# One attention and FP4 feed-forward layer on one core: a new order for the setup

## What is computed

```python
xn = (x - mean(x)) / sqrt(var(x) + 1e-5)            # by rows
q, k, v = split(xn @ w_attn + b_attn)               # 16 heads of 8
scores = q @ k.T / sqrt(8) + mask                   # mask: -log(1 + distance) ahead, -inf behind
attn = (softmax(scores) @ v) @ w_proj + b_proj
def fp4(t):                                         # blocks of 16 along the last axis
    scale = max(max(abs(block)) / 6, 1e-12)
    return grid[searchsorted(mid, abs(block / scale))] * sign * scale
h = silu(fp4(xn) @ fp4(w_gate).T) * (fp4(xn) @ fp4(w_up).T)
out = x + attn + fp4(h) @ fp4(w_down).T
```

## Time and profile before

| what | value |
|---|---|
| median of 3 runs | 626.64 us (626.51 to 628.41) |
| profiled execution, its own time | 626.35 us |
| its span, first to last instruction | 624.5 us |
| mean granted TensorE clock | 0.985 |
| busy PE, DVE, POOL, ACT | 564.4 (90%), 562.8 (90%), 537.4 (86%), 400.8 (64%) us |
| chain that ended last, by engine | PE 43%, POOL 32%, DVE 13%, ACT 7%, issue 4% |

### The profile page before, as it was taken

The page is one execution under the profiler, slowest core; times in us unless marked ns, Lnnn a source line. Parts: engine busy times, 40 slices in busy tenths (PEclk is TensorE's granted clock), DMA queues, the critical chain, the costliest instruction groups (busy, mean ns, idle before and its releaser), DMA issues.

```text
span 624.5 us, 11270 instructions
## 1 busy us (share of the span) xinstructions
PE 564.4 (90%) x3807; PEld 250.9 (40%) x3807; DVE 562.8 (90%) x1178; ACT 400.8 (64%) x857; POOL 537.4 (86%) x400
## 2 busy tenths in 40 slices
PE   6999779999999999999989899999989898989985
PEld 5576534444343334333333332342334242432322
DVE  6899998989999999999999999998989999997661
ACT  4576457566656475767667577666656667759782
POOL 7226987789899989999998999999998999998992
PEclk9999988999999999999999999999999999999997
DMA  5255341310000000200000000000000000000000
GB/s 148 74 137 114 119 83 51 78 43 36 2 2 3 0 2 10 86 1 2 2 0 2 19 1 1 2 2 1 1 2 1 19 0 2 1 2 1 1 2 17
DMA packets 14715, 16.66 MB, mean 27 GB/s; under 512 B 1594, under 2 KB 14171, under 8 KB 14243
## 3 DMA queue, kind: packets, MB, share of 16 engines
q1 hardware_dynamic: 14123, 15.70, 9.2%
q10 hardware_dynamic: 536, 0.26, 0.2%
HBM read 11.75 MB, written 4.01 MB: 25 GB/s over the span
## 4 chain that ended last, share of the span: by engine, by line
PE 43%; POOL 32%; DVE 13%; ACT 7%; issue 4%; ACTq 0%; POOLq 0%; DVEq 0%
POOL ring L802 25%; PE psum L1396 11%; PE psum L1354 9%; PE psum L1378 7%; DVE mxp L1135 7%; ACT ring L954 2%; POOL xw L820 2%; POOL xw L818 2%; PE psum L1331 2%; POOL xw L822 2%; PE psum L1312 2%; PE psum L1314 1%; PE psum L1320 1%; DVE ring L1162 1%; PE psum L1404 1%
## 5 line engine op out<-in xcount | busy, mean ns | idle before, releaser
L802 POOL TENSOR_TENSOR ring<-ring,dist 128x1024 f32<-128x1024 f32 (+3 forms) x223 | 438.4, 1996 | 31.7 <-ACT ring L954 31.3
L1135 DVE TENSOR_REDUCE mxp<-psum 128x1 f32<-128x512 f32 (+3 forms) x640 | 352.6, 598 | 20.5 <-PE psum L1354 11.4
L954 ACT ACTIVATE ring<-psum 128x512 f32<-128x512 f32 (+3 forms) x446 | 211.5, 528 | 101.5 <-PE psum L1381 51.9
L1354 PE MATMUL psum<-kop,qop 96*128 96x512 bf16 (+3 forms) x640 | 198.0, 352 | 7.3 <-DVE mxp L1135 5.3
L1378 PE MATMUL psum<-qop,kop 128*128 128x512 bf16 (+3 forms) x640 | 190.7, 349 | 6.2 <-DVE mxp L1135 3.7
L1396 PE MATMUL psum<-ring,vaug 128*32 128x512 f32 (+3 forms) x1280 | 151.5, 544 | 15.0 <-POOL ring L802 14.1
L1162 DVE TENSOR_TENSOR ring<-psum,dist 128x512 f32<-128x512 f32 (+3 forms) x194 | 115.7, 622 | 13.9 <-ACT psum L954 13.8
L954 ACT ACTIVATE psum<-psum 128x512 f32<-128x512 f32 (+3 forms) x194 | 99.5, 543 | 39.7 <-PE psum L1378 23.4
L1354 PEld LDWEIGHTS psum<-kop,qop 96*128 96x128 bf16 x640 | 57.2, 97 | 127.8 <-DVE mxp L1135 46.5
L1378 PEld LDWEIGHTS psum<-qop,kop 128*128 128x128 bf16 x640 | 59.7, 97 | 82.2 <-DVE mxp L1135 15.5
L1357 PE MATMUL psum<-tri_q,identb 128*128 128x128 bf16 x256 | 56.2, 221 | 0.0
(11 more groups left out here) (130 smaller groups left out, 490.2 us busy)
## 6 DMA issues: line engine op xcount, KB each, us to landing
kop<-parts_dram SPq DMA_DIRECT2D x9, 384.0 KB
qop<-parts_dram SPq DMA_DIRECT2D x9, 384.0 KB
parts_dram<-qpart SPq DMA_DIRECT2D x18, 128.0 KB, 2.8
xin<-_attn_hidden_states_dram SPq DMA_DIRECT2D x4, 256.0 KB, 4.7
ring<-inv_dram SPq DMA_DIRECT2D x1, 1024.0 KB, 4.9
out_dram<-xin SPq DMA_DIRECT2D x4, 256.0 KB, 2.3
parts_dram<-qpart SPq DMA_DIRECT2D x6, 96.0 KB
qop<-parts_dram SPq DMA_DIRECT2D x3, 192.0 KB
```

Source lines behind the costliest of these rows:

```text
L802: g_.tensor_tensor(slot(p)[:, :, 0:n], slot(p)[:, :, 0:n], both, ALU.mult).then_inc(weighed_pool, 1)
L954: a_.activation(scores if pair_vec[p] else slot(p)[:, e % 2, 0:n], scores, ACT.Exp, scale=SCALE).then_inc(exp_done, 1)
L1135: v_.tensor_reduce(mxp[:, u % 2, 4 * a + j, c - g:c - g + 1], bank(*o)[:, 0:n], AX_X, ALU.max).then_inc(max_used, 1)
L1354: ins = mm(bank(*o)[:, 0:n], qop[0:K_MAX, u // NQ % 2, h, P * a:P * (a + 1)], kop[0:K_MAX, h, k0:k0 + n], start=True, stop=(c != g))
```

## The change

1. **Square root first.** `qzero(0)` on ACT now needs `sqrt(0)`, so the root is ACT's first activation.
2. **Row scales once.** The four small instructions of `scale` run for chunk 0 of the order and once, 12 columns wide, for the other three. `scale` of chunks 2 and 3 of the order is then only the four that write rows.
3. **Rests in PSUM.** For the first chunk DVE's two subtractions and ACT's second part work on the product's PSUM bank in place of the SBUF tile `qc`.
4. **Scales padded.** `amax` and `sc` are 35 columns for each piece, and stage 1 always writes all 35 through a view of 5 by 7, from a flat 35. DVE clears `amax` once at the start.
5. **Order.** FP4 piece 0 waits for the last `rest`. The selection products of heads 1 to 3, `scale`, `dist` and `v` get other ranks, the first unit's maxima are walked head by head, FP4 stages 3 to 5 get a rank of their own, and the plan lets some DVE items start only after POOL's running one. `WARM` is 20 in place of 30.
6. **Clearings in quarters.** `qzero(1)` and `kfill` of chunks 1 to 3 are four ACT instructions each; POOL's clearing of the weights' tile comes last of its constants.

```diff
-WARM = 30
+WARM = 20
+DIST_RANK, V_RANK, SEL_RANK, SCALE_RANK = 8, 8, 4.3, 4.5
+PORT_RANK = 6.8
...
-    add("ACT", ("qzero", 0), 2700, 200, [], rank=0)
+    add("ACT", ("qzero", 0), 2700, 200, [("ACT", ("sqrt", 0))], rank=0)
...
+            needs += [("DVE", ("rest", 1, 1))] if n == k == 0 else []
...
-        for a in range(TPG):
-            for j in range(4):
+        for a, j in sorted(((a, j) for a in range(TPG) for j in range(4)), key=lambda o: o[1] if u == 0 else 0):
...
+        if engine == "DVE" and (kind == "fp4" and item[2] >= 3 or kind == "scale" or item[0:3:2] == ("rest", 1)):
+            now = max(now, clock["POOL"] if pool_busy[0] else 0)
...
-                    a_.activation(qpart[:, t, 1], rest(t), ACT.Identity).then_inc(part2_ready, 1)
+                    a_.activation(qpart[:, t, 1], rest(t) if ci else bank("qk", 0, t),
+                                  ACT.Identity).then_inc(part2_ready, 1)
...
-                vec.wait_ge(std_ready, 1 if ci == 0 else 2)
-                seq(v_.reciprocal(st1[:, 4, tiles], st1[:, 3, tiles]))
...
+                tiles = slice(TPG * CHUNKS[0], NT) if ci == 0 else slice(0, TPG * CHUNKS[0])
+                if ci < 2:
+                    vec.wait_ge(std_ready, ci + 1)
+                    seq(v_.reciprocal(st1[:, 4, tiles], st1[:, 3, tiles]))
...
-                    ins = v_.tensor_scalar(sc[:, of], amax[:, of], 1.0 / 6.0, 1e-12, ALU.mult, ALU.max)
+                    ins = v_.tensor_scalar(sc[:, n].rearrange("p (a b) -> p a b", b=7), amax[:, n],
+                                           1.0 / 6.0, 1e-12, ALU.mult, ALU.max)
...
-                        v_.scalar_tensor_tensor(out=rest(t), in0=bank("qk", 0, t), scalar=bqk[:, t:t + 1],
+                        v_.scalar_tensor_tensor(out=bank("qk", 0, t), in0=bank("qk", 0, t), scalar=bqk[:, t:t + 1],
...
-                        v_.tensor_tensor(qpart[:, t, 2], rest(t), qpart[:, t, 1], ALU.subtract).then_inc(part3_vec, 1)
+                        v_.tensor_tensor(qpart[:, t, 2], bank("qk", 0, t), qpart[:, t, 1],
+                                         ALU.subtract).then_inc(part3_vec, 1)
```

More of the change, by code:

```diff
@@ L31 @@
 XW = S + 6 * P + F
-NB = XW // BLK
+SC_COLS = 35
 WHALF = (XW - S) // 2
@@ L117, in plan @@
             add("ACT", ("sqrt", ci), 200, 100, [("DVE", ("stats", ci))], rank=0)
-        add("DVE", ("scale", ci), 2000, 100, [("ACT", ("sqrt", 0 if ci == 0 else NG - 1))], at=at, rank=1 if ci < 2 else 3)
+        add("DVE", ("scale", ci), (2800, 2000, 1400, 1400)[ci], 100, [("ACT", ("sqrt", 0 if ci == 0 else NG - 1))],
+            at=at, rank=SCALE_RANK if ci else 1)
         pe(("xnT", ci), 8 * P, [("DVE", ("scale", ci))], rank=1)
@@ L141, in plan @@
         for t in range(2):
-            pe(("sel", t, h), PARTS * GQ, [("DVE", ("rest", t, 1)), ("POOL", ("consts",))], rank=1)
+            pe(("sel", t, h), PARTS * GQ, [("DVE", ("rest", t, 1)), ("POOL", ("consts",))], rank=SEL_RANK if h else 1)
         vec(("sel", 0, h), GQ, [("PE", ("sel", 0, h))], rank=0)
@@ L145, in plan @@
     for k in range(NG):
-        pe(("dist", k), 4 * GQ, [("DMA", ("hankel",)), ("POOL", ("consts",))] + first, rank=4)
+        pe(("dist", k), 4 * GQ, [("DMA", ("hankel",)), ("POOL", ("consts",))] + first, rank=DIST_RANK)
         act(("dist", k), GQ, [("PE", ("dist", k))], rank=3)
@@ L273, in released @@
         if kind == "qk":
-            by = ("DVE", ("rest", o[2], 0)) if o[1] == 0 else ("ACT", ("qf",) + o[1:])
+            by = ("DVE", ("rest", o[2], 1)) if o[1] == 0 else ("ACT", ("qf",) + o[1:])
         if kind == "st":
@@ L325, in take @@
         kind = item[0]
+        if engine == "DVE" and (kind == "fp4" and item[2] >= 3 or kind == "scale" or item[0:3:2] == ("rest", 1)):
+            now = max(now, clock["POOL"] if pool_busy[0] else 0)
+        if engine == "POOL":
+            pool_busy[0] = kind != "consts"
         end = now + took + drain + SEEN
@@ L392, in plan @@
     idle = 0
+    pool_busy = [False]
     while True:
@@ L413, in plan @@
         if best is None:
-            others = [clock[e] for e in busy if clock[e] > now]
+            if engine == "POOL":
+                pool_busy[0] = False
+            others = [clock[e] for e in busy if e != engine]
             step = min([t for t in (soonest, min(others) if others else None) if t is not None] or [now + 100])
```

63 lines of the change are left out of this document (34 added, 29 removed).

## The result

The changed kernel takes 625.46 us in the median (624.67 to 626.09), the kernel before 627.18 us beside it: a ratio of 0.9972, interval 0.9963 to 0.9981. That is 1.7 us faster, a gain that is small but clear of the noise, and 8 us above the forecast of 617.2. Its profiled execution took 624.67 us, with a span of 622.8 us and a mean granted clock of 0.992. Over all of it DVE is busy for 562.4 us, where it was 562.8 before: what the change took off DVE came back elsewhere.

What follows compares the result with a forecast made beforehand. DVE, POOL and PE, all near their limit in the long middle, were taken as the bound. Setup terms of -9.4 us took the span from 624.5 to 615.1 us, forecast 617.2 us (614.5 to 619.5), wider range 611.5 to 622.5.

Steps and rivals of the forecast that it cites:

- The start: First chunk's setup and first unit: transposes at 9.2 us, selection near 17.2, unit 0's maxima near 32.3, -5.9 us.
- Rival 5: Setup: TensorE, with fewer fillers, loses its clock from 10 to about 30 us: 632 us; chance 0.04.
- The sum up to unit 4: DVE's account to unit 4's end at 113.59 us: -5.9 + 2.8 + 0.5 - 3.2 - 3.6 = -9.4 us.
- Scales: Four DVE scales drop from 958 ns to 0.17 us in the 5 by 7 form: -3.2 us.
- Rival 2: The new scale form is held up by POOL all the same, PE's wait near 75 us stays: 620.4 us; chance 0.08.
- Contention: FP4 piece 0's DVE stages, moved among the maxima, may meet POOL there: +0.5 us, between 0 and +2.2.
- Idle time: Up to unit 4, a remainder: DVE's 1.84 us at the second root goes, PE's 4.21 us wait shrinks; -1.7 us.
- Weighings: Six of the 18 weighings before unit 4's milestone go from DVE to POOL: counted as zero, between -2.7 and +2.
- rival 1: Only the start arrives; DVE's savings from 60 to 113 us wait for PE and POOL: 621.2 us; chance 0.16.
- The middle hands an earlier start on at par: The middle, its work being the same, passes the -9.4 us on whole: span 624.5 to 615.1 us.
- rival 3: More than the sum: two steps of transposed scores move from tail into gaps of the middle: 612.6 us; chance 0.14.
- Rival 4: Every later item has another neighbour, so waits of the new order could add up to the gain: 626 us; chance 0.05.

Runs made afterwards that it cites:

- sc_pitch: The changed kernel with all orders kept and the block maxima written with a pitch of 8 columns: 625.63 us, ratio 0.9965.
- splice4_rows_pitch: Changed kernel to unit 4's combining, then the order of before; last two chunks' rows written near 30 us, maxima at pitch 8: 624.6 us, ratio 0.995.
- section 1: The experiments' first section, on which DVE forms POOL holds up; its one run is forms.
- rows_early: The changed kernel, order kept, with the rows of all three later chunks written at once behind the second root, POOL idle: 623.64 us, ratio 0.9955.
- splice4: The changed kernel up to unit 4's combining, from there the order of before on PE, DVE, ACT and POOL: 625.99 us, ratio 0.9981.
- delay_before: The kernel before, orders kept, with five repeats of VectorE's 1.74 us fill ahead of the first chunk's statistics: 631.93 us, ratio 1.0084.
- forms: A separate small kernel, each DVE form four times beside POOL multiplications and again alone: 5 by 7 view 4.87 us beside POOL, pitch of 8 0.86.

## Why the prediction was wrong

**The start** was right in each term: transposes -3.35 us (forecast -3.5), selection row at 17.23 (17.2), unit 0 at 32.13 (32.3). Rival 5 can go: the clock stood at 1.00 from 10 to 40 us, in each stretch of 10 us.

**The sum up to unit 4** was -9.4 us and came out as -2.48 us. DVE's account up to that point, busy time by kind from its windows, line by line (0 to 113.59 us and 0 to 111.11 us):

| | before | after | change | forecast |
|---|---|---|---|---|
| subtractions of the first chunk | 4.25 | 2.88 | -1.4 | -1.4 |
| small row scale instructions | 4.77 | 1.53 | -3.2 | -3.6 |
| scales of FP4 | 4.59 | 4.27 | -0.3 | -3.2 |
| row writes | 6.82 | 9.27 | +2.5 | |
| exponent and rounding passes | 7.35 | 9.53 | +2.2 | |
| blocked multiplies | 7.13 | 5.66 | -1.5 | |
| these three together | | | +3.2 | +0.5 |
| weighings | 7.84 | 5.36 | -2.5 | 0 |
| maxima | 44.70 | 45.60 | +0.9 | 0 |
| idle, less overlaps | 6.13 | 6.80 | +0.7 | -1.7 |
| all else | | | +0.2 | 0 |

(The forecast of idle time is what is left of -9.4 when its other terms are taken off. The rows of neighbouring instructions overlap a little: the kinds add up to 107.5 us in before, and DVE is busy for 100.7. So the last line but one is less than DVE's idle time.) Four terms were mis-sized:

- *Scales, -3.2.* It came out as -0.3. Rival 2 had the mechanism, not the time (620.4 us): the new form is held up all the same, 712 ns in the mean of six. The prediction drew on a rule of the Trainium skill there (VectorE: DVE Perf Modes, What auto-detection actually checks), and set 5 against 35. The trace doesn't agree with that reading: the view of 35 columns in a row behaves as a flat one, and only a gap in memory, the pitch of 8, takes it out of the hold (0.86 for 4.87 us). The rule itself isn't refuted: if the view is merged, it has 35 against 35, which are equal, and the pitched form has 5 against 35. But a form that isn't held would have gained next to nothing: 0 us in `sc_pitch`, 0.9 in `splice4_rows_pitch`.
- *Contention, +0.5.* It came out as +3.2 (row writes, passes and multiplies together), and was counted for FP4 piece 0 only. But every row write and exponent pass is a form that POOL holds (section 1), and whether it meets POOL is a matter of the microsecond. Moving the work ahead of them by 3 to 7 us dealt new meetings, among them 4.89 us for the last chunk's rows. `sc_pitch` showed why taking off one meeting may give nothing: 3.2 us less in the scales came back as 2.6 in the passes and waits behind them and 0.6 in its own maxima.
- *Idle time, -1.7.* It came out as +0.7. The prediction expected PE's wait for the last rows to shrink, and with it the slow clock. It stayed (3.62 us for 4.21), since the four row writes alone took 4.89 us, where the small instructions and the writes together had taken 5.11 (2.77 + 2.34); `rows_early` shows that the rows were its cause.
- *Weighings, 0.* They were -2.5 us at unit 4, and no gain: `splice4` leaves the six with POOL for good, has all other work done as before at unit 5, and stands at +0.32, since DVE waits for PE and POOL there. That is the mechanism of rival 1, that what DVE alone saves waits for the other two; its price (621.2 us) was too good.

The step that failed is thus the addition itself: savings of DVE before unit 4 were added at par to the shift of the start. The runs show holds beside POOL and waits for PE and POOL in their place, and by unit 5 nothing is left of the savings or of the shift (`splice4`, +0.32 us where -9.4 were forecast for unit 4).

**"The middle hands an earlier start on at par"** was right where the order is kept (`delay_before`, `splice4`), and no help for an order that is planned anew. From unit 5 to 15 the changed order lost 6.5 us more on DVE (-1.69 to +4.76) and was 6.5 us shorter in the tail behind the last maxima (62.1 us before, 55.6 after). That fits rival 3's mechanism, with two steps of scores gone from the tail as it said (4.6 us by its price); it forgot that DVE and POOL have no room for them in the middle, as the earlier trace rows shows. The two nearly cancel.

**Rival 4** ("the middle eats it", 626 us) named the time and the wrong place. What spoke against it in the prediction, that no rule for the middle had changed, was also false: the rule for an idle engine had.

One thing the prediction didn't price at all. The forecast and every rival took the order of before as typical. Neighbours of it are up to 8 us slower, and a re-planned kernel draws again. The range of 611.5 to 622.5 us left no room for that. So it is in part luck that the changed kernel is faster at all: one of its four neighbours takes 633 us.

What stays open: how much of the difference between the two families of plans is the change's, and how much the luck of a few draws; and which of DVE's meetings with POOL one could avoid together.

## What to carry to other kernels

Where a planner or a scheduler sets the order, time a few plans that differ by nothing (a duration off by 1 ns) before you credit a change of the setup with a per cent: here they spread over 10 us. Then test the change with the order held fixed, and compare at a point where both orders have done the same work; a milestone at which work was only put off flatters. And before you move DVE work to avoid POOL, list which forms are held up, and move them to where POOL is idle; taking out one alone may only pass the hold to the next (that taking out all that stand in a row pays wasn't tried).

## What the hardware showed that was not expected

- A view of 5 by 7 over contiguous memory is no view: 1.22 us each beside POOL, the same as flat, and 0.21 with a pitch of 8.
- The price of a hold grows far less than the instruction held. Beside POOL multiplications of 2.47 us each (83.86 by 34) it is 1.0 us more for each scale of 35 columns (4.87 less 0.83, by 4), 1.9 for each row write of 128 (9.19 less 1.50) and 2.0 for each subtraction of 512 (10.95 less 2.87). In the changed kernel one scale of 35 columns lost 1.9 us (2.04 for 0.17).
- Row writes, once clear of POOL, take 0.26 us each (3.17 us for twelve), and beside it 1.22 (4.89 for four) in the changed kernel and 2.30 (9.19 for four) in `forms`: the place of an instruction was worth more than its work.
